# GpSimd's scatters in the first stage wait for the attention scores to leave TensorE

## The chip, the core and the metric

The kernel runs on one NeuronCore of one Trainium2 chip. A core has five engines with a queue of instructions each: TensorE (PE; its weight loads are a row of their own, PEld), VectorE (DVE), ScalarE (ACT), GpSimd (POOL) and SyncE (SP), which here only starts DMAs. Engines meet through semaphores: an instruction waits until a counter has reached a value, and every instruction behind it in the same queue waits with it. The metric is device time in microseconds of one launch; the time before is a median of three runs.

## The reference

The input `x` is 8192 tokens of 128 features (128 graphs of 64 nodes), `adj` a 64 x 64 matrix per graph.

```python
x = x + gnn0(layernorm(x), adj)            # adj @ (x @ W) + b
x = x + ffn0(layernorm(x))                 # attention, then a mixture of 8 experts
x = x + gnn1(layernorm(x), adj_normalised)
x = x + ffn1(layernorm(x))                 # 6 experts, top 2 of them

# inside ffn0, for every graph of 64 tokens, 4 heads of 32
scores = einsum("bhtd,bhsd->bhts", q, k) / sqrt(32)      # causal mask, softmax
x = x + (softmax(scores) @ v) @ wo.T
flat = rmsnorm(x)                          # root of the mean of squares
weights = top2(softmax(flat @ router_w.T)) # 2 of 8 experts for each token
out = sum over experts of weights * (silu(flat @ w1.T) * (flat @ w3.T)) @ w2.T
```

The first stage of the kernel computes everything up to `flat` and the choice of two experts for each token, and then copies every token's row of `flat` to two places in HBM, one for each expert chosen. The second stage runs the experts over those rows in blocks of 256. The third stage gathers the results and computes `gnn1` and `ffn1`.

## The kernel before

The tokens are cut into 16 groups of 512 (`NG = 16`), each of 4 tiles of 128. The first stage is a software pipeline written by hand: `sweep` (line 227 onwards holds the stage) runs a body 23 times on each engine, and in pass `i` the body works on group `i - k` for several depths `k` at once; `g[5]` in it means group `i - 5`. Each engine has its own list of steps and goes through them strictly in that order. Semaphores `at["name"]` say that step `name` of a group has ended, and `upto(name, n)` is the value that says so for the first n groups.

The steps that matter, by engine:

- TensorE, in order of a pass: `pk` (part of the projections to queries and keys, line 831), `prT` (transposes, line 901), `v` (line 871), `gnn` (lines 809 and 812), `rank` (lines 956 to 959), `y` (attention times values, 32 small matmuls of 64 x 66, line 919), `scores` (4 matmuls with the mask, line 885, then 64 small ones of 32 x 64, line 891), `hT` (line 823), `yT` (line 928), `gnnT` (line 796), `wo` (line 938), `pqs`, `pks`, `pq` (line 831).
- VectorE: `rden` and `yn` (lines 603 and 611, from `y`), `slot` (line 713, the rows in HBM that a group's tokens go to), `max` and `sub` (lines 589 and 597, first the maximum of the scores, then its subtraction), `lg` (line 642, needs `wo`), `nmr` (line 550, needs `rstd1`), `f2` (line 629), `topi` (line 656), `qks` and `qkc` (line 561), `ssv` (line 636, mean of squares), `qkr` (line 584). `max` waits for `scores`; `v` on TensorE waits for `qks`.
- ScalarE: `flat` (line 444, needs `rms`), `vd` (lines 402 to 405), `yTc` (line 426), `prTc` (line 419) among others.
- GpSimd: `rstd1` (line 314) and `rms` (line 319), two roots written as powers, and eight scatters for each group (line 329). One scatter is an indirect DMA that writes 128 rows of 512 bytes to the places that `slot` lists.

GpSimd's body runs in this order in pass `i`: scatters 2 and 5 of group `i - 6`, `rms` of group `i - 5`, scatters 1 and 7 of group `i - 6`, scatter 0 of group `i - 5` (the first of that group, which waits for its `flat` and `slot`), `rstd1` of group `i - 1`, scatters 3, 6 and 4 of group `i - 5`. The root that `nmr` needs therefore stands behind three scatters.

The last group's eight scatters are issued in the second stage, whose instructions start behind a barrier that all engines reach at the end of the first (line 227 and line 1274 in the order below).

Of the kernel before, what the change touches and what calls it, by code (L numbers as in the profile page):

```python
# [25 lines left out]
NG = TOK // GT  # L26
# [55 lines left out]
def signals(sem, names):  # L82

    return {n: sem(n) for n in names.split()}
# [12 lines left out]
def build(nc, x, adj_t, gnn0_w, gnn0_b, ln1, ln2, wqkv, wo, router0, w13, w2, gnn1_w, gnn1_b,  # L97
# [19 lines left out]
    with ExitStack() as whole:  # L117
# [31 lines left out]
        with ExitStack() as ctx:  # L149
# [51 lines left out]
            def upto(n, groups):  # L201

                return step_of[n].at(n, groups - 1)

            at, step_of = {}, {}
# [3 lines left out]
            def sweep(body):  # L209

                for i in range(NG + DEEP):
                    body([i - k if 0 <= i - k < NG else None for k in range(DEEP + 1)], [b for b in range(len(LN)) if LN_AT[b] == i])

            def tiles(a, g):

                return a[:, g * TG:(g + 1) * TG]
# [10 lines left out]
            with nc.Block() as block:  # L227
# [49 lines left out]
                @block.gpsimd  # L277
                def _(pool):
                    for i in range(2):
                        G.memset(adjt[i][:, :, :], 0.0).then_inc(zeroed, 1)  # L280
                        if i == 0:
                            G.memset(mhalf[:, :], -0.5).then_inc(pool_w, 1)
                            G.memset(one_raw[:, :], 0.0).then_inc(pool_w, 1)
                            G.memset(halves[:, :], 0.0).then_inc(pool_w, 1)
                    G.memset(zrow[:, :], 0.0).then_inc(zeroed, 1)
                    pool.wait_ge(pool_w, 3)
                    pool.wait_ge(zeroed, 3)
                    G.memset(one_raw[0:1, :], 1.0).then_inc(pool_w, 1)
                    pool.wait_ge(pool_w, 4)
                    G.memset(halves[0:NN, 7:8], 1.0).then_inc(pool_w, 1)  # L290
                    pool.wait_ge(pool_w, 5)
                    G.memset(one_raw[NN // 2:NN // 2 + 1, :], 1.0).then_inc(pool_w, 1)
                    pool.wait_ge(pool_w, 6)
                    G.memset(halves[NN:P, 15:16], 1.0).then_inc(pool_w, 1)
                    pool.wait_ge(pool_w, 7)
                    G.memset(sel_all[:, 0, TG, :], 0.0).then_inc(pool_w, 1)
                    G.memset(v_diag[:, :, :, :], 0.0).then_inc(pool_w, 1)
                    pool.wait_ge(pool_w, 9)
                    G.memset(v_diag[0:NN, :, :, 32:33], 1.0).then_inc(pool_w, 1)
                    pool.wait_ge(pool_w, 10)  # L300
                    G.memset(v_diag[NN:P, :, :, 65:66], 1.0).then_inc(pool_w, 1)
                    pool.wait_ge(pool_w, 11)

                    def ln_pow(bs):

                        for b in bs:
                            pool.wait_ge(at["ln_var"], upto("ln_var", b + 1))
                            s = slice(LN[b][0] * TG, (LN[b][-1] + 1) * TG)
                            G.tensor_tensor(rs_a[:, s], var_a[:, s], mhalf[:, s], ALU.pow).then_inc(at["ln_pow"], 1)

                    def rstd1(g):
                        if g is not None:
                            pool.wait_ge(at["var1"], upto("var1", g + 1))
                            G.tensor_tensor(rs_b[:, g, :, :], var_b[:, g, :, :], mhalf[:, 0:2 * TG].rearrange("p (k t) -> p k t", k=2), ALU.pow).then_inc(at["rstd1"], 1)

                    def rms(g):
                        if g is not None:
                            pool.wait_ge(at["ssv"], upto("ssv", g + 1))
                            G.tensor_tensor(tiles(rr2, g), tiles(ssv, g), mhalf[:, 0:TG], ALU.pow).then_inc(at["rms"], 1)

                    def scatter(n, g):

                        if g is not None and g < NG - 1:
                            if n == 0:
                                if g == 0:
                                    pool.wait_ge(zero_fill, 16 * (NDUM + NE0))
                                pool.wait_ge(at["flat"], upto("flat", g + 1))
                                pool.wait_ge(at["slot"], upto("slot", g + 1))
                            G.indirect_dma_start(  # L329
                                out=slots_in, out_offset=bass.IndirectOffsetOnAxis(ap=slot_now0[g % 2][:, n:n + 1], axis=0),  # L330
                                in_=flat[g % 2][:, n // 2, :], in_offset=None, bounds_check=ROWS - 1).then_inc(scattered[g % 2], 16)

                    def body(g, new):
                        ln_pow(new)
                        scatter(2, g[6])
                        scatter(5, g[6])
                        rms(g[5])
                        scatter(1, g[6])
                        scatter(7, g[6])
                        scatter(0, g[5])  # L340
                        rstd1(g[1])
                        scatter(3, g[5])
                        scatter(6, g[5])
                        scatter(4, g[5])
                    sweep(body)

                @block.scalar
# [678 lines left out]
        with ExitStack() as ctx:  # L1026
# [34 lines left out]
            upto = x2[:, :, :].rearrange("p t c -> p (t c)")[:, 0:MB * 8].rearrange("p (j e) -> p j e", e=8)  # L1061
# [40 lines left out]
            at = signals(sem, "pick held add0 add1 st0 mv0 var0 rstd0 scale xn xb aT tT gnn x3 "  # L1102
                              "st1 mv1 var1 rstd1 f3 f3T hi lo rh rhr logits "
                              "etop ep gateT gTc eb oTc oT ob")
# [1205 lines left out]
```

## Time and profile before

| | us |
|---|---|
| time, median of 3 runs (lowest to highest) | 863.1 (862.56 to 863.46) |
| profiled execution: span from first to last instruction | 932.6 |
| first stage in it | 0 to about 315 |
| second stage in it | about 315 to 590 |
| third stage in it | about 590 to 932 |
| TensorE busy in the span | 846.5 (91%) |
| GpSimd busy in the span | 433.0 (46%) |

The span is the profiled execution's own time on the core; the page gives none for what lies around it, so that the span alone stands beside the median. Every instruction of that execution left a record, which is not so in the runs that were timed. A start is when the engine began an instruction; an instruction that sat waiting has its idle time in square brackets, with what ended it: an engine and line, "remote" where nothing of this core in the trace fits, "issue" where nothing in it was waited for. The end of a matmul is modelled and not measured.

### The profile page before, as it was taken

How to read it: one execution, taken by the hardware profiler on the slowest of the kernel's cores; microseconds unless marked ns; L12 is line 12 of the kernel's file. 1: busy time of each engine (PE TensorE's matmuls, PEld its weight loads, DVE VectorE, ACT ScalarE, POOL GpSimd, SP SyncE). 2: the span in 40 equal slices, each digit the busy share in tenths (PEclk: the TensorE clock that was granted, in tenths of full speed). 3: DMA queues.
4: the chain of work that ended last, by engine and by line, in shares of the span. 5: the costliest groups of instructions: out<-in, count | busy, mean ns of one | idle time of the engine just before them, and what ended most of it. 6: DMA issues, size and time to landing. Idle time of an engine off the chain costs nothing.

```text
span 932.6 us, 21565 instructions
## 1 busy us (share of the span) xinstructions
PE 846.5 (91%) x6286; PEld 649.8 (70%) x6287; DVE 698.3 (75%) x2699; ACT 515.8 (55%) x1072; POOL 433.0 (46%) x410
## 2 busy tenths in 40 slices
PE   7988898989866499999999998999998999999998
PEld 6656676766643399999999998755665555555564
DVE  5898777767743499887777786988887778777763
ACT  3666666756532355665666554456555555545554
POOL 3258777668744630092010022366665556656400
PEclk9999989989977799999999999999999999999999
DMA  9504211131000376666666674144333333433322
GB/s 252 158 24 106 67 41 41 44 99 41 31 23 26 109 205 181 174 181 182 172 172 161 168 182 114 43 141 151 118 115 114 107 107 122 135 112 132 121 80 90
DMA packets 104712, 108.25 MB, mean 116 GB/s; under 512 B 27279, under 2 KB 88673, under 8 KB 102465
## 3 DMA queue, kind: packets, MB, share of 16 engines
q1 hardware_dynamic: 94096, 88.52, 33.3%
q0 software_dynamic: 8880, 18.19, 6.5%
q8 instruction: 36, 0.59, 0.3%
q10 hardware_dynamic: 1664, 0.66, 0.3%
q14 instruction: 36, 0.29, 0.1%
HBM read 82.07 MB, written 25.26 MB: 115 GB/s over the span
## 4 chain that ended last, share of the span: by engine, by line
PE 52%; issue 6%; DVE 3%; POOL 2%; another core or an unknown queue 1%; ACT 1%; DVEq 0%; POOLq 0%; ACTq 0%
PE banks L2041 15%; PE banks L2081 10%; PE banks L2207 7%; PE banks L2199 6%; PE banks L2175 5%; PE banks L2056 2%; PE banks L2113 2%; POOL expert_rows L1336 1%; PE banks L2102 1%; PE banks L2221 1%; PE banks L2130 1%; PE banks L2151 1%; PE banks L2122 1%; PE banks L2142 1%
## 5 line engine op out<-in xcount | busy, mean ns | idle before, releaser
L1336 POOL DMA_INDIRECT expert_rows<-slots_out,slot_c x128 | 143.8, 1124 | 80.9 <-DVE ys L1580 45.0
L329 POOL DMA_INDIRECT slots_in<-flat,slot_now x120 | 123.3, 1027 | 46.8 <-issue 34.6
L2041 PE MATMUL banks<-xT_hi,w_hi 128*128 128x256 f32 (+1 forms) x426 | 126.1, 296 | 0.7 <-issue 0.4
L2041 PE MATMUL banks<-xT_hi,w_lo 128*128 128x256 f32 (+1 forms) x426 | 120.1, 282 | 0.0
L2041 PE MATMUL banks<-xT_lo,w_hi 128*128 128x256 f32 (+1 forms) x426 | 119.8, 281 | 0.0
L2081 PE MATMUL banks<-w_sb,prod 128*128 (+1 forms) x852 | 106.7, 274 | 0.0
L2081 PEld LDWEIGHTS banks<-w_sb,prod 128*128 128x128 f32 (+1 forms) x852 | 101.0, 191 | 0.5 <-issue 0.2
L2041 PEld LDWEIGHTS banks<-xT_hi,w_hi 128*128 128x128 f32 (+1 forms) x426 | 75.6, 177 | 1.4 <-issue 1.4
L2041 PEld LDWEIGHTS banks<-xT_lo,w_hi 128*128 128x128 f32 (+1 forms) x426 | 75.8, 178 | 0.0
L2041 PEld LDWEIGHTS banks<-xT_hi,w_lo 128*128 128x128 f32 (+1 forms) x426 | 75.6, 177 | 0.0
L1401 ACT ACTIVATE w_hi<-w_raw 128x684 fp32r<-128x684 f32 x71 | 54.9, 773 | 29.1 <-PE banks L2041 24.5
L1410 ACT ACTIVATE xT_hi<-banks,ln 128x256 fp32r<-128x256 f32 x71 | 33.7, 474 | 57.0 <-PE banks L2056 56.3
L2175 PE MATMUL banks<-f_hi,ew_hi 128*128 128x512 f32 x96 | 64.2, 669 | 0.4 <-ACT h L1427 0.2
L831 PE MATMUL banks<-hT,wq 128*128 128x512 f32 x128 | 61.6, 622 | 2.7 <-DVE sc L597 2.7
L1599 DVE TENSOR_TENSOR w_lo<-w_raw,w_hi 128x684 fp32r<-128x684 f32 x71 | 63.0, 888 | 0.0
L1361 POOL TENSOR_TENSOR rs_d<-var_d,mhalf 128x4 f32<-128x4 f32 x16 | 17.9, 1121 | 93.8 <-DVE var_d L1744 93.8
L1434 ACT ACTIVATE flat<-banks,eb 128x512 f32<-128x512 f32 x64 | 43.8, 687 | 23.6 <-DVE ys L1772 15.6
L1416 ACT ACTIVATE act<-banks 128x512 f32<-128x512 f32 x71 | 42.6, 600 | 20.8 <-PE banks L2041 18.7
L1346 POOL TENSOR_TENSOR xb_c<-x,gb 128x512 f32<-128x512 f32 x16 | 20.6, 1285 | 70.5 <-DVE x L1672 70.1
L1608 DVE TENSOR_TENSOR prod<-banks,act 128x512 f32<-128x512 f32 x71 | 48.9, 688 | 0.3 <-PE banks L2041 0.3
L891 PE MATMUL banks<-qk_rot 32*64 32x64 f32 x1024 | 31.3, 239 | 19.3 <-issue 19.3
L589 DVE TENSOR_REDUCE mx<-banks 128x16 f32<-128x1024 f32 x16 | 19.5, 1222 | 37.5 <-remote 21.2
(303 smaller groups left out, 2187.9 us busy)
## 6 DMA issues: line engine op xcount, KB each, us to landing
f_all<-gates_dram SPq DMA_DIRECT2D x16, 1536.0 KB
w_raw<-in_w SPq DMA_DIRECT2D x71, 342.0 KB
xs<-slots_in SPq DMA_DIRECT2D x71, 128.0 KB
slots_out<-ys SPq DMA_DIRECT2D x71, 128.0 KB
base_all<-in_x SPq DMA_DIRECT2D x16, 256.0 KB, 4.2
out<-ob SPq DMA_DIRECT2D x16, 256.0 KB
slots_in<-zrow SPq DMA_DIRECT2D x20, 128.0 KB
adjt<-in_adj_t SPq DMA_DIRECT2D x32, 64.0 KB
```

The source lines that it names most:

```text
L329: G.indirect_dma_start(out=slots_in, out_offset=bass.IndirectOffsetOnAxis(ap=slot_now0[g % 2][:, n:n + 1], axis=0), in_=flat[g % 2][:, n / ...
L831: T.matmul(banks[bank][:, :], wq[:, n * P:(n + 1) * P], hT[:, :], start=True, stop=True).then_inc(done, 1)
L1336: G.indirect_dma_start(out=rows[p][:, n, :], out_offset=None, in_=slots_out[0:filled(g) * R, :], in_offset=bass.IndirectOffsetOnAxis(ap=sl ...
L1401: S.activation(w_hi[:, u % 2, :], w_raw[:, u, :], ACT.Copy).then_inc(w_hi_done, 1)
L1434: S.activation(h2[n % 3][:, :], banks[B_B[n]][:, :], ACT.Relu, bias=eb2[:, n:n + 1]).then_inc(per["rb"].sem, 1)
L1599: V.tensor_tensor(w_lo[:, u % 2, :], w_raw[:, u, :], w_hi[:, u % 2, :].bitcast(f32), ALU.subtract).then_inc(w_lo_done, 1)
L1608: V.tensor_tensor(prod[:, par, 0:2, :].rearrange("p c r -> p (c r)"), banks[3 + 3 * par][:, :], act1[:, par, 0:2, :].rearrange("p c r -> p ...
L2041: last = T.matmul(banks[bank][0:m, half * R:(half + 1) * R], ww[:, par, n * HIDP + c * P:n * HIDP + c * P + m], xx[:, par, :], start=q == ...
L2081: last = T.matmul(banks[7][:, t * P:(t + 1) * P], prod[0:widths[c], par, c, t * P:(t + 1) * P], w2_sb[0:widths[c], bass.ds(e * (KC * C) + ...
L2175: last = T.matmul(banks[B_A[n]][:, :], ww[:, w], ff[p][:, :], start=q == 0, stop=q == 2)
L2199: T.matmul(banks[B_B[n]][:, :], ew2[:, n * C:(n + 1) * C], h1[n % 3][:, :], start=True, stop=True).then_inc(per["b"].sem, 1)
L2207: T.matmul(banks[B_C][:, :], ew3[:, n * C:(n + 1) * C], h2g[n % 3][:, :], start=n == 0, stop=False).then_inc(per["c"].sem, 1)
```

## The change

A new step `behind_scores` is called between `rms` and the two scatters 1 and 7. In pass `i` it makes GpSimd wait until the `scores` step of group `i - 3` has ended (of the last group, once `i - 3` is past it). Nothing else is edited, and no instruction is added that computes or moves data.

```diff
+                    def behind_scores(g):
+
+                        if g is not None and g < NG - 1:
+                            pool.wait_ge(at["scores"], upto("scores", min(g + 3, NG - 1) + 1))
+
                     def body(g, new):
                         ln_pow(new)
                         scatter(2, g[6])
                         scatter(5, g[6])
                         rms(g[5])
+                        behind_scores(g[6])
                         scatter(1, g[6])
                         scatter(7, g[6])
                         scatter(0, g[5])
```

GpSimd's queue in the middle of the stage, one pass from `rms` on, first before the change (`rr` is written by `rms`, `rs_b` by `rstd1`; the brackets name semaphores waited for):

```order
L319 TENSOR_TENSOR rr<-ssv,mhalf 128x4 [waits at_ssv]
L329 DMA slots_in<-flat,slot_now 69632x128 x2
L329 DMA slots_in<-flat,slot_now 69632x128 [waits at_slotf,at_flat]
L314 TENSOR_TENSOR rs_b<-var_b,mhalf 128x8 [waits at_mv1]
L329 DMA slots_in<-flat,slot_now 69632x128 x5
```

The same pass after the change:

```order
L319 TENSOR_TENSOR rr<-ssv,mhalf 128x4 [waits at_ssv]
L329 DMA slots_in<-flat,slot_now 69632x128 [waits at_scores]
L329 DMA slots_in<-flat,slot_now 69632x128
L329 DMA slots_in<-flat,slot_now 69632x128 [waits at_slotf,at_flat]
L314 TENSOR_TENSOR rs_b<-var_b,mhalf 128x8 [waits at_mv1]
L329 DMA slots_in<-flat,slot_now 69632x128 x5
```

No instruction has moved against another; the first scatter behind `rms` has a wait, and the two scatters, the third one, `rstd1` and five more scatters are queued behind it.

GpSimd's queue at the end of the stage, where `rstd1` has no group left, before:

```order
L319 TENSOR_TENSOR rr<-ssv,mhalf 128x4 [waits at_ssv]
L329 DMA slots_in<-flat,slot_now 69632x128 x2
L329 DMA slots_in<-flat,slot_now 69632x128 [waits at_slotf,at_flat]
L329 DMA slots_in<-flat,slot_now 69632x128 x5
L319 TENSOR_TENSOR rr<-ssv,mhalf 128x4 [waits at_ssv]
L329 DMA slots_in<-flat,slot_now 69632x128 x2
L227 UNCONDITIONAL_BRANCH
L1274 UNCONDITIONAL_BRANCH [waits barrier_Pool_Activation_PE_DVE_SP_gather]
```

And after:

```order
L319 TENSOR_TENSOR rr<-ssv,mhalf 128x4 [waits at_ssv]
L329 DMA slots_in<-flat,slot_now 69632x128 [waits at_scores]
L329 DMA slots_in<-flat,slot_now 69632x128
L329 DMA slots_in<-flat,slot_now 69632x128 [waits at_slotf,at_flat]
L329 DMA slots_in<-flat,slot_now 69632x128 x5
L319 TENSOR_TENSOR rr<-ssv,mhalf 128x4 [waits at_ssv]
L329 DMA slots_in<-flat,slot_now 69632x128 [waits at_scores]
L329 DMA slots_in<-flat,slot_now 69632x128
L227 UNCONDITIONAL_BRANCH
L1280 UNCONDITIONAL_BRANCH [waits barrier_Pool_Activation_PE_DVE_SP_gather]
```

The order is again the same. In the last two passes the wait names scores that ended a pass or more earlier; in the two passes ahead of them it names the scores of the last two groups.

## Rows read from the trace of the kernel before

**Rows 1.** The page's head: span, and number of instructions recorded.

```profile
span 932.6 us, 21565 instructions
```

**Rows 2.** Stretches: length; busy us of PE, PEld, DVE, ACT, POOL (instructions); clock, DMA.

```profile
0.00:330.00 330.00, 269.91 (x2746) 201.71 (x2748) 225.56 (x974) 181.11 (x479) 202.55 (x194) 0.89 0.27 78
330.00:592.00 262.00, 258.91 (x2227) 257.88 (x2227) 213.82 (x445) 151.62 (x274) 52.86 (x52) 0.99 0.63 167
592.00:933.00 341.00, 317.68 (x1317) 190.23 (x1315) 258.94 (x1282) 183.10 (x320) 177.59 (x166) 0.99 0.36 114
```

**Rows 3.** Waits: who, for whom, us in total, times, longest.

```profile
ACT tT_c L1441 <- remote: 26.2, 8, 3.6
DVE mx L589 <- remote: 21.2, 2, 10.8
DVE mx L589 <- PE banks L891: 16.3, 6, 3.6
DVE rden L603 <- remote: 7.8, 5, 1.7
```

**Rows 4.** Timeline, TensorE, group 1: start, us, engine, line, operation, count.

```profile
39.98 1.01 PE L871 MATMUL banks<-wq,hT 128*128 128x72 f32 x8
...
44.11 0.91 PE L891 MATMUL banks<-qk_rot 32*64 32x64 f32 x64
```

**Rows 5.** Timeline, 203 to 222 us: scores of group 11, and what follows.

```profile
205.59 1.05 POOL L329 DMA_INDIRECT slots_in<-flat,slot_now  x1 [0.20 <-issue]
...
206.60 0.57 PE L891 MATMUL banks<-qk_rot 32*64 32x64 f32 x18
...
206.94 0.97 POOL L329 DMA_INDIRECT slots_in<-flat,slot_now  x1 [0.30 <-issue]
...
207.59 0.36 PE L891 MATMUL banks<-qk_rot 32*64 32x64 f32 x6 [0.42 <-issue]
...
208.33 0.74 PE L891 MATMUL banks<-qk_rot 32*64 32x64 f32 x40 [0.38 <-issue]
...
208.37 0.26 DVE L603 RECIPROCAL rden<-banks 128x16 f32<-128x16 f32 x1 [1.68 <-remote]
...
209.90 0.97 POOL L329 DMA_INDIRECT slots_in<-flat,slot_now  x1 [1.99 <-DVE slot_now L713]
...
210.89 1.68 POOL L314 TENSOR_TENSOR rs_b<-var_b,mhalf 128x8 f32<-128x8 f32 x1
...
212.61 0.16 DVE L550 SCALAR_TENSOR_TENSOR nmr<-mv_b,rs_b 128x4 f32<-128x4 f32 x1
...
214.75 1.21 DVE L561 TENSOR_TENSOR qk_sin<-banks,cst 128x1024 f32<-128x1024 f32 x1
...
216.37 1.01 PE L871 MATMUL banks<-wq,hT 128*128 128x72 f32 x8
```

**Rows 6.** Timeline, 247 to 294 us: scores of group 14, and the tail.

```profile
247.09 0.97 POOL L329 DMA_INDIRECT slots_in<-flat,slot_now  x1 [0.30 <-issue]
...
247.18 1.04 PE L901 MATMUL banks<-cst,pr 128*128 128x128 f32 x8
...
248.26 1.03 ACT L419 ACTIVATE prT<-banks 128x1024 f32<-128x1024 f32 x1 [0.60 <-issue]
...
252.41 0.94 PE L891 MATMUL banks<-qk_rot 32*64 32x64 f32 x43
...
252.45 1.05 POOL L329 DMA_INDIRECT slots_in<-flat,slot_now  x1 [0.20 <-issue]
...
261.48 0.97 POOL L329 DMA_INDIRECT slots_in<-flat,slot_now  x1 [0.30 <-issue]
...
263.93 1.23 DVE L589 TENSOR_REDUCE mx<-banks 128x16 f32<-128x1024 f32 x1 [10.80 <-remote]
...
293.45 1.04 POOL L319 TENSOR_TENSOR rr<-ssv,mhalf 128x4 f32<-128x4 f32 x1 [7.61 <-DVE ssv L636]
```

**Rows 7.** One line's instructions: duration ns min/median/max, first and last start, shape.

```profile
L329 POOL DMA_INDIRECT slots_in<-flat,slot_now x120: 968/975/1808, 60.4 to 310.9; - x120
```

## The prediction

> **What bounds the kernel now.** I read the head of the page first, against the times. The recorded execution spans 932.6 us [rows 1]; the median of the timed runs is 863.1, which is 69.5 less. So before any term is priced it has to be known which part of the trace the timed runs don't have.
>
> The stretches come next. TensorE is busy for 258.91 of 262 us in the second stretch and for 317.68 of 341 in the third [rows 2]. If the timed runs keep just that busy time, 576.6 us, they have at most 863.1 - 576.6 = 286.5 us for the first 330: at least 43.5 us of the first stretch is in the record only.
>
> The timeline of the first stage shows what that can be. Where no scatter is near, the 64 score matmuls take 0.91 us [rows 4]. In group 11 they start at 206.60 and end at 209.07, with two gaps of "issue", while GpSimd scatters; VectorE and ScalarE stand still, and `rden` comes 1.68 us late for a `y` that had ended before the scores began [rows 5]. In group 14 eight scatters run back to back from 252.45 to 262.45; 43 score matmuls go at full pace, and `max` starts at 263.93, after 10.80 us of waiting, once the last scatter is over [rows 6]. The table of waits adds this up: `max` waited 21.2 + 16.3 us and `rden` 7.8, together 45.3 us [rows 3]. That is nearly the 43.5 missing from the same stretch. The third stage has the like, 26.2 us, where ScalarE waits beside the gathers [rows 3].
>
> Is it the scatter alone that holds TensorE's signals back? No: at 247.09 one is under way, eight transposes end at 248.22, and ScalarE picks them up at 248.26 [rows 6]. What sets the scores apart is their density: 64 matmuls and as many weight loads, 128 records, in 0.91 us. I conclude, and no row proves it, that the stall is one of writing records while GpSimd issues DMAs, and that the timed runs have little of it.
>
> The Trainium skill, "NOTIFIC — the notification-queue block", section 7.1, speaks for that: the block that takes the records is set up so that its inner pipeline holds its producers back rather than lose one. By that rule the scores' stall goes with the recording and the sum below stands.
>
> The Trainium skill, "Runtime: NRT & Kernel Launch", section "The ~15µs preamble/postamble breakdown", speaks against it: a profile's total is about 6.2 us above the reported time for any kernel. By it the timed runs would hold nearly all the stalls. Here the gap is 69.5 us, so the measurement decides against the figure; the mechanism it implies is the first rival.
>
> **The change, part by part.** Nothing is computed or moved that was not before; one wait is added in each of 15 passes. Behind it in GpSimd's queue stand scatters 1 and 7, scatter 0, `rstd1`, five scatters and the next `rms`. VectorE's `nmr` waits for `rstd1`, and behind `nmr` stand `f2`, `qks`, `qkc` and `qkr`; TensorE's `v` waits for `qks`. That is the path on which the wait costs.
>
> Let s be the end of the scores.
>
> *After.* The first scatter starts about 0.20 after what released it, takes 1.05, the next two 0.30 + 0.97 each [rows 5, 7]: the third ends at s + 0.20 + 1.05 + 1.27 + 1.27 = s + 3.8. `rstd1` takes 1.68 and `nmr` follows by 0.04 [rows 5]: s + 5.55.
>
> *Before, without the stall.* Group 11's scores would end at 206.60 + 0.91 = 207.51. Everything behind the late `rden` moves up by its 1.68, so `nmr` at 212.61 becomes 210.93 [rows 5]: s + 3.4. The wait makes `nmr` 2.1 us late.
>
> *What of it is hidden.* `qk_sin` starts 2.14 after `nmr` and ends at 215.96, `v` starts at 216.37: TensorE was last there by 0.4, and that much lateness costs nothing [rows 5]. The rest is on the path.
>
> *The period of a group.* From `v` to the scores takes 44.11 - 39.98 = 4.13 [rows 4]; that group has no `rank`, for which I add 0.2. After: 5.55 + 2.14 + 1.21 + 0.05 + 4.3 + 0.91 = 14.15. Before, by the same path: 3.4 + (216.37 - 212.61) + 4.3 + 0.91 = 12.4. But GpSimd's own pass is longer than that: eight scatters 1.28 apart, 1.68 for `rstd1`, 1.05 for `rms` make 12.9 [rows 5 to 7]. I take 12.9. Each period grows by 14.15 - 12.9 = 1.25 us. The bounds: 1.75, if GpSimd runs a little faster than its records, and 0, if in the timed runs something unseen already makes the period 14.15.
>
> *How often.* `rstd1` stands behind the wait for groups 5 to 15. For group 5 the code still has statistics of new input between `max` and `sub` on VectorE, which I take to cover it. Ten periods remain: 12.5 us.
>
> *The tail.* In the last passes there is no `rstd1`; the wait only moves scatters. In group 14 the first one goes from 252.45 to 252.41 + 0.94 + 0.20 = 253.55, 1.1 us later [rows 6]. GpSimd is idle for 7.61 us before `rms` at 293.45 [rows 6], which looks like cover; but that idle time is there because `max` was 10 us late. Without the stall VectorE is ready before GpSimd is through its eight scatters, GpSimd's queue leads to the barrier at the stage's end, and the 1.1 us stays: 1 us, with bounds 0 and 2.
>
> *What it removes.* Scores that meet no scatter: worth at most the 45.3 us in the record, and by the above next to nothing in the timed runs. I take 0; the other end is in the first rival.
>
> Sum for the timed runs: 863.1 + 12.5 + 1 = 876.6, so 876.5. Sum against the profiled execution's own 932.6: there the stall is real, and goes. Of its 45.3 us the last `max` waited 21.2 - 10.8 = 10.4 [rows 3], but behind it GpSimd's eight scatters lead once the stall is gone: the `rms` at 293.45 can come earlier by its idle 7.61 less the 1.1 alone, 6.5 us, so 3.9 of the 10.4 are not given back. That makes 932.6 - 41.4 + 13.5 = 904.7. So the forecast is that the span falls by some 28 us while the time rises by 13.5.
>
> **The rivals.**
>
> *The stall is real in the timed runs.* For it: the record shows it where scores meet scatters, in the middle of the stage and in its tail [rows 5, 6], and the change takes away just that. Against it: the 43.5 us that the first stage must lose. If all of it were real the time would be 863.1 - 28 = 835. The turning point: with a share f of the 41.4 us real, the change gains as soon as 41.4 f is over 13.5, so from f = 0.33. By the stretches f is at most (45.3 - 43.5) / 45.3, under 0.1 [rows 2, 3], unless TensorE's modelled busy time in the other stages is itself stretched. Half real gives 863.1 - 20.7 + 13.5 = 856.
>
> *The lateness is hidden.* If GpSimd's scatters follow each other faster when nothing is recorded, `rstd1` is ready for `nmr` anyway. To bring 5.55 down to 3.4 + 0.4 the three scatters must shrink from 3.6 to 1.85 us, about half; 968 ns is the least in 120 records [rows 7], which speaks against it. Or VectorE or ScalarE bounds the period already. Time: 863 to 864.5.
>
> *The wait runs on into ScalarE.* GpSimd is through its five scatters at s + 5.5 + 0.2 + 6.4 = s + 12.1 and `rms` ends at 13.15. `flat` and the four `vd` copies follow on ScalarE ahead of `yTc`, which `wo` needs. That leaves them 1.0 us until the next scores end at 14.15, and `yTc` is wanted soon after. Nothing in the rows says how much of that is short; at half of the 1.0 us in ten groups, 5 us come on top: 882.
>
> **How the numbers follow.** The forecast with its third rival, which has the same sign, gets 0.70; its own range is ten times 0.5 to 1.75 plus 0 to 2, and some of the 5, so 868 to 885. The real stall gets 0.17, the hidden lateness 0.13. What a measurement of this kernel can tell from no change is about 0.2%, 1.7 us: faster 0.17, same 0.13, slower 0.70. The range of 861 to 885 takes in the forecast, the hidden lateness and the mildest of the real stall.
>
> **What would show it.** In the changed kernel's profile: score matmuls of every group in about 0.9 us without gaps; `max` soon after them in the last two groups; the first scatter behind `rms` waiting for the scores; `nmr` waiting for `rstd1` for 1 to 2 us in each middle group, where group 11's shows no wait now [rows 5]; a span near 905. A span that falls beside a time that rises would confirm that the stall was the recording's. I am wrong if the time falls below 861: then the scatters do hold the scores back in the timed runs too. I am also wrong if `nmr` finds `rstd1` ready, whatever the time.

## The result, and the profile after

The changed kernel takes 885.1 us (median of 4 runs, 882.5 to 888.7) against 863.3 (4 runs, 862.6 to 868.3): a ratio of 1.025, interval 1.021 to 1.029, so it is slower by some 22 us. The forecast was 876.5. The direction and the place were right, the size 9 us short: the time stands at the upper end of the range of 861 to 885.

The profiled execution of the changed kernel took 882.45 us, 2.05 more than its span of 880.4. It recorded 21565 instructions, as before. Its stretches, which answer to [rows 2], the first one cut 1.75 us behind the start of the first stage's last scatter (length; busy us of PE, PEld, DVE, ACT, POOL with instructions; granted clock of TensorE as a share of 2.4 GHz; DMA share; GB/s):

```profile
0.00:284.00 284.00, 233.88 (x2681) 172.88 (x2682) 215.11 (x946) 172.96 (x467) 186.73 (x177) 0.94 0.28 80
284.00:553.00 269.00, 263.57 (x2247) 261.45 (x2248) 218.52 (x455) 157.43 (x282) 64.14 (x66) 0.99 0.64 172
553.00:880.00 327.00, 319.38 (x1360) 194.74 (x1358) 262.39 (x1299) 184.60 (x324) 176.41 (x167) 1.00 0.37 120
```

The span fell by 52 us while the time rose by 22. The record of before is therefore no yardstick for the change; the first experiment replaces it.

The table of waits no longer has `max` waiting 21.2 + 16.3 us, `rden` 7.8, nor the third stage's `tT_c` behind a remote releaser [rows 3]. One entry is new and one has grown (who, line, for whom: us in total, times, longest; the second stood at 0.3 us in the first record of before and at 3.6 in the second, below):

```profile
POOL slots_in L329 <- PE banks L897: 23.3, 12, 4.0
...
DVE nmr L556 <- POOL rs_b L314: 17.5, 10, 3.0
```

The first is the added wait, the second its effect: ten times, as the forecast counted, VectorE stands before `nmr` until GpSimd has the root. One period of the timeline shows both (start, length, engine, line, operation; in brackets the idle time before it and its releaser; lines behind 329 are 6 higher than in before):

```profile
197.59 0.91 PE L897 MATMUL banks<-qk_rot 32*64 32x64 f32 x64
...
199.32 1.05 POOL L329 DMA_INDIRECT slots_in<-flat,slot_now  x1 [1.51 <-PE banks L897]
...
200.68 0.97 POOL L329 DMA_INDIRECT slots_in<-flat,slot_now  x1 [0.30 <-issue]
...
201.95 0.97 POOL L329 DMA_INDIRECT slots_in<-flat,slot_now  x1 [0.30 <-issue]
...
202.76 0.19 DVE L648 TENSOR_TENSOR lg<-banks,v_logits 128x32 f32<-128x32 f32 x1 [1.26 <-PE banks L944]
...
202.95 1.68 POOL L314 TENSOR_TENSOR rs_b<-var_b,mhalf 128x8 f32<-128x8 f32 x1
...
204.65 0.17 DVE L556 SCALAR_TENSOR_TENSOR nmr<-mv_b,rs_b 128x4 f32<-128x4 f32 x1 [1.70 <-POOL rs_b L314]
...
206.78 1.21 DVE L567 TENSOR_TENSOR qk_sin<-banks,cst 128x1024 f32<-128x1024 f32 x1
...
208.05 1.11 PE L877 MATMUL banks<-wq,hT 128*128 128x72 f32 x8 [1.02 <-DVE qk_sin L567]
...
212.40 0.91 PE L897 MATMUL banks<-qk_rot 32*64 32x64 f32 x64
```

Read it downwards as a chain: the scores end at 198.50, the first scatter starts 0.82 later, the third ends at 202.92, the root at 204.63, `nmr` follows 0.02 behind it, then the sine, then `v` on TensorE, which waits for the sine, then the next scores at 212.40. The period is 14.81 us, and groups 7 to 13 repeat it within 0.02. The scores meet no scatter and take 0.91, against 2.47 with two gaps in [rows 5].

### The profile page after: what moved, and what is told of

It is laid out like the page before. It is cut to its first block, busy times and chain, and to the rows that moved or that the text cites. A ratio compares the mean times of both kernels' runs of the same rounds, so it can differ in the third digit from the quotient of the medians.

```text
span 880.4 us, 21565 instructions
## 1 busy us (share of the span) xinstructions
PE 816.8 (93%) x6286; PEld 629.1 (71%) x6287; DVE 696.0 (79%) x2699; ACT 515.0 (58%) x1072; POOL 427.3 (49%) x410
## 4 chain that ended last, share of the span: by engine, by line
PE 62%; issue 2%; DVE 1%; POOL 1%; ACTq 0%; ACT 0%; POOLq 0%; DVEq 0%
PE banks L2047 16%; PE banks L2087 10%; PE banks L2213 9%; PE banks L2205 9%; PE banks L2181 7%; PE banks L2062 2%; PE banks L2119 2%; PE banks L2108 1%; PE banks L2136 1%; PE banks L2227 1%; PE banks L2148 1%; PE banks L2128 1%; PE banks L2157 1%; POOL expert_rows L1342 1%; PE banks L2219 0%
## 5 line engine op out<-in xcount | busy, mean ns | idle before, releaser
L329 POOL DMA_INDIRECT slots_in<-flat,slot_now x120 | 125.9, 1049 | 58.4 <-issue 34.8
L1586 DVE COPY ys<-banks 128x256 f32<-128x256 f32 x71 | 29.9, 421 | 23.2 <-PE banks L2087 22.8
L1602 DVE SCALAR_TENSOR_TENSOR xT_lo<-banks,ln,xT_hi 128x256 fp32r<-128x256 f32 x71 | 34.2, 482 | 16.6 <-ACT xT_hi L1416 16.4
```

The costliest lines, as they stand in the source:

```text
L329: G.indirect_dma_start(out=slots_in, out_offset=bass.IndirectOffsetOnAxis(ap=slot_now0[g % 2][:, n:n + 1], axis=0), in_=flat[g % 2][:, n / ...
```

## The experiments

Below, s is the end of a group's score matmuls.

### The kernel before, recorded again

> The kernel before once more, for a second recorded execution. If the stalls of the scores belonged to that one recorded execution, this one has score matmuls of 0.91 us in every group, a period near 12.9 us in the middle of the first stage and a span near 861. If every recorded execution has them, the span is near 930 again with the scores at 2.5 to 5 us. The time is near 863 either way.

It took 867.2 us with a span of 865.2. The same program, so no edit; and the long stalls of the first record are gone, though the scores don't come down to 0.91 nor the period to 12.9:

```profile
186.57 1.40 PE L891 MATMUL banks<-qk_rot 32*64 32x64 f32 x64
...
186.95 1.05 POOL L329 DMA_INDIRECT slots_in<-flat,slot_now  x1 [0.19 <-issue]
...
190.57 1.68 POOL L314 TENSOR_TENSOR rs_b<-var_b,mhalf 128x8 f32<-128x8 f32 x1
...
192.28 0.16 DVE L550 SCALAR_TENSOR_TENSOR nmr<-mv_b,rs_b 128x4 f32<-128x4 f32 x1 [0.38 <-POOL rs_b L314]
...
195.81 1.01 PE L871 MATMUL banks<-wq,hT 128*128 128x72 f32 x8
...
197.10 1.22 DVE L584 TENSOR_TENSOR qk_rot<-qk_cos,qk_sin 128x1024 f32<-128x1024 f32 x1
...
197.62 1.55 POOL L329 DMA_INDIRECT slots_in<-flat,slot_now  x1 [0.30 <-issue]
...
199.19 1.05 POOL L319 TENSOR_TENSOR rr<-ssv,mhalf 128x4 f32<-128x4 f32 x1
...
200.05 1.40 PE L891 MATMUL banks<-qk_rot 32*64 32x64 f32 x64
```

Beside a scatter the scores take 1.40 us: 0.49 more than alone, not 1.5 or 10 more. `nmr` comes at s + 4.31 and waits 0.38; the period is 13.48. What sets it can be followed in these rows. GpSimd has no idle time but the 0.2 to 0.3 between instructions, and VectorE none that the view shows between `nmr` and `qkr`. From one `rms` (at 185.71) to the end of the root behind the three scatters are 6.54 us, then 0.03 to `nmr`, 4.82 to `qkr`, 1.22 for `qkr`, 0.85 from its end to the end of the scatter ahead of the next `rms`, and 0.02: together 13.48. Neither the scores nor `v` are in this ring. `v` doesn't wait for the sine here, and behind the scores TensorE waits another 0.58 us for `vd`. The stretches, the first again cut 1.7 us behind the start of the last scatter, say what is left to compare with the changed kernel:

```profile
0.00:268.00 268.00, 230.32 (x2681) 170.97 (x2682) 216.06 (x946) 173.86 (x467) 187.94 (x177) 0.96 0.30 85
268.00:537.00 269.00, 263.46 (x2239) 261.09 (x2240) 217.63 (x453) 156.73 (x280) 63.73 (x66) 0.99 0.65 172
537.00:865.00 328.00, 320.17 (x1368) 195.92 (x1367) 263.35 (x1302) 185.31 (x325) 176.37 (x167) 1.00 0.37 119
```

The last two stretches are 597 us here and 596 in the changed kernel, the first is 268 and 284: the whole difference between the kernels is made in the first stage, 16 us in these two records. 41 timed runs of before, beside the experiments, had spans between 859.4 and 866.8; none was near 932.6. That execution was the exception. The recorded executions of this run (867.2) and of the changed kernel (882.45, the shortest of its four) are themselves among the timed ones, so what the text ahead of the prediction says of the timed runs, that not every instruction leaves a record, does not hold for them: recording does not stretch a program so in general.

### The root's place, without the wait

```diff
                         scatter(0, g[5])
-                        rstd1(g[1])
                         scatter(3, g[5])
                         scatter(6, g[5])
+                        rstd1(g[1])
                         scatter(4, g[5])
```

> The kernel before, without any wait for the scores, but with rstd1 two scatters later in GpSimd's pass (behind scatter 6 instead of scatter 0). GpSimd's pass is as long as before. Theory A: nmr comes 2.5 us later, near 6 us after the scores' end, the period is some 14.5 us and the time about 879. Theory B: the late root costs nothing, as GpSimd loses no time: 863 to 865.

Made in the kernel before, this costs nearly all that the change costs: 881.7 us, ratio 1.020 (1.016 to 1.024). No wait is added, the scores still may meet scatters, and `nmr` now waits for the root:

```profile
DVE nmr L550 <- POOL rs_b L314: 25.9, 11, 3.1
```

So a late root is enough to make a loss of this size. It is more than the ten even steps I expected: the periods alternate, 13.7 and 17.8, and this is not the root alone. In a short pass `v` to scores takes 4.35 us at the full granted clock; in the long one, where TensorE had waited 2.26 us for the sine, it takes 7.31 at a mean of 0.53, nearly all of it at the 1.2 GHz level:

```profile
194.72:199.07 4.35, 4.35 (x59) 3.69 (x59) 4.35 (x15) 2.83 (x8) 3.08 (x3) 1.00 0.46 179
209.75:217.06 7.31, 7.31 (x58) 6.31 (x58) 4.95 (x20) 3.70 (x10) 4.48 (x4) 0.53 0.09 29
```

So 3 us of every second pass are the slower clock. How much of the 881.7 the lateness alone would make, this run does not say.

### The root straight behind the wait

```diff
                         behind_scores(g[6])
+                        rstd1(g[1])
                         scatter(1, g[6])
                         scatter(7, g[6])
                         scatter(0, g[5])
-                        rstd1(g[1])
```

> The changed kernel with rstd1 straight behind the wait, ahead of the three scatters. Theory A (the wait costs because rstd1 stands three scatters behind it, so that nmr is late): nmr is ready by 3.4 us after the scores' end again, the period goes back to about 13 and the time to about 865. Theory B (the wait costs because GpSimd's pass is full: rms ends later, and flat, the vd copies and yTc on ScalarE with it): rms still ends some 14 us after the last scores, the period is 14.3 instead of 14.8, and the time about 880.

The time stays, and theory A's 865 does not come: 882.5 us, ratio 1.023 (1.018 to 1.027). The root is early, `nmr` at s + 3.10 in every second pass, but the passes between are long: periods of 12.25 and 18.45, a mean of 15.35. In the long ones VectorE stands in front of `lg`, the step ahead of `nmr`, and waits for `wo`:

```profile
195.97 1.05 POOL L319 TENSOR_TENSOR rr<-ssv,mhalf 128x4 f32<-128x4 f32 x1
...
197.05 1.28 ACT L450 ACTIVATE flat<-f_all,rr 128x128 f32<-128x128 f32 x4 [3.91 <-POOL rr L319]
...
201.70 2.02 PE L944 MATMUL banks<-wo_sb,yT 128*128 128x136 f32 x8
...
203.76 0.19 DVE L648 TENSOR_TENSOR lg<-banks,v_logits 128x32 f32<-128x32 f32 x1 [5.24 <-PE banks L944]
203.86 0.15 DVE L556 SCALAR_TENSOR_TENSOR nmr<-mv_b,rs_b 128x4 f32<-128x4 f32 x1
```

This is the chain of my third rival (the root of the sum of squares, then `flat`, `vd`, `yTc`, `wo`). With eight scatters behind the root it is what comes last. The clock has a part here too: the granted clock is 0.82 over the long pass and 1.00 over the short one, and `wo` takes 2.02 us in place of 1.15. So moving the root forward is no cure, and the rival is real, though not what the changed kernel shows, where `lg` at 202.76 is done 1.7 us before `nmr` can start.

### The wait in the tail alone

```diff
-                        if g is not None and g < NG - 1:
+                        if g is not None and NG - 5 <= g < NG - 1:
                             pool.wait_ge(at["scores"], upto("scores", min(g + 3, NG - 1) + 1))
```

> The changed kernel with the wait only in the last four passes that have it (scatter groups 11 to 14), where rstd1 has no group behind it. Theory A: 1.1 us of GpSimd's tail, time about 864. Theory B: GpSimd is full in the tail as well and its end sets the stage's end, 865 to 867. If most of the loss were in the tail, it would be near 880.

864.6 us (10 runs), ratio 1.002 (1.000 to 1.005): 0 to 4 us, near the 1 us of the forecast. From the end of group 13's scores to the last scatter's start it took 53.0 us, against 51.4 in the second record of before: 1.6 more with the wait.

### One scatter less behind the wait

```diff
-                        behind_scores(g[6])
                         scatter(1, g[6])
+                        behind_scores(g[6])
                         scatter(7, g[6])
```

> The changed kernel with the wait one scatter later: scatter 1 goes ahead without it, 7 and 0 and all behind them wait for the scores. Theory A, the price is the root's lateness: scatter 7 starts 0.8 us behind the scores, 0 at s+2.2, the root at s+3.2 and nmr at s+4.9, where the kernel before has 4.3 and the changed one 6.15. The scores meet one scatter and take about 1.2 in place of 1.40. The period is 13.48 + 0.6 - 0.2 - 0.1 = 13.8, and the time 863 + 10 x 0.3 + 1 = 867, ratio 1.004 (1.001 to 1.009). Rival, the wait itself costs (queue restarted once a pass, whatever stands behind it): nearly the whole 22 us stay, 880 or more. Rival, scores that meet no scatter were worth something that only the full wait brings: then this one is as good as before or faster, 858 to 863.

869.9 us, ratio 1.0088 (1.0071 to 1.0105): within the interval given, at its upper end. `nmr` is where theory A put it, 4.79 behind the scores; the scores keep their 1.41 us, where I had expected 1.2: one scatter beside them costs as much as before.

```profile
185.88 1.41 PE L897 MATMUL banks<-qk_rot 32*64 32x64 f32 x64
...
186.30 1.05 POOL L329 DMA_INDIRECT slots_in<-flat,slot_now  x1 [0.20 <-issue]
...
188.09 0.97 POOL L329 DMA_INDIRECT slots_in<-flat,slot_now  x1 [0.74 <-ACT flat L450]
...
190.37 1.68 POOL L314 TENSOR_TENSOR rs_b<-var_b,mhalf 128x8 f32<-128x8 f32 x1
...
192.08 0.16 DVE L556 SCALAR_TENSOR_TENSOR nmr<-mv_b,rs_b 128x4 f32<-128x4 f32 x1 [0.83 <-POOL rs_b L314]
...
199.82 1.40 PE L897 MATMUL banks<-qk_rot 32*64 32x64 f32 x64
```

The view names `flat` as releaser of the scatter at 188.09; it starts 0.80 behind the scores' end, as behind the added wait elsewhere. The rival that the wait itself costs (880 or more) is out: the wait is there in each pass, and two thirds of the loss are gone.

### A shorter root, in both kernels

`nmr` needs only half of the 8 columns; the other half gives a ratio close to 1, here the first term of its series on VectorE:

```diff
-    G.tensor_tensor(rs_b[:, g, :, :], var_b[:, g, :, :], mhalf[:, 0:2 * TG]..., ALU.pow)
+    G.tensor_tensor(rs_b[:, g, 1, :], var_b[:, g, 1, :], mhalf[:, 0:TG], ALU.pow)
...
-    V.reciprocal(tiles(inv_h, g), rs_b[:, g, 1, :])
+    V.reciprocal(tiles(inv_h, g), var_b[:, g, 0, :])
...
-    V.tensor_tensor(tiles(ratio, g), rs_b[:, g, 0, :], tiles(inv_h, g), ALU.mult)
+    V.tensor_scalar(tiles(ratio, g), tiles(inv_h, g), -0.5e-5, 1.0 + 0.5e-6, ALU.mult, ALU.add)
```

In the kernel before:

> The kernel before with rstd1 on 4 columns instead of 8 (the other root follows from the first through a reciprocal and one VectorE operation in place of another; with the variances here it agrees to single precision). Theory A': GpSimd's pass, which shows no idle time in the second recorded execution of the kernel before, sets the period of 13.48 us, so 0.62 us less for the root gives 12.86, ten times: 857. Rival: TensorE's own chain of about 13.4 us sets it: 863.

861.9 us (10 runs), ratio 0.9964 (0.9942 to 0.9986): a gain of 1 to 5 us, less than expected, and the only version here that beats both kernels. `nmr` is 0.53 earlier, the period 13.09, 0.39 shorter for a root that is 0.63 shorter; then `nmr` no longer waits for the root, but `lg` ahead of it for `wo`, and the gain ends:

```profile
189.12 0.19 DVE L642 TENSOR_TENSOR lg<-banks,v_logits 128x32 f32<-128x32 f32 x1 [0.85 <-PE banks L938]
189.23 0.20 DVE L550 SCALAR_TENSOR_TENSOR nmr<-mv_b,rs_b 128x4 f32<-128x4 f32 x1
```

In the changed kernel:

> The changed kernel, with the root on 4 columns in place of 8 (the other half, which only feeds a ratio, comes from a reciprocal on VectorE). Theory A, the loop scores, scatters 1, 7, 0, root, nmr, sine, v, scores sets the period: the root is 0.47 us shorter (as it was in the kernel before: nmr 1.24 behind the root's start in place of 1.71), nmr at s+5.7, the period 14.80 - 0.47 = 14.3, and over eleven periods some 5 us off the changed kernel's 885: 880, ratio 1.019. Rival B, GpSimd's whole pass with the root of the sum of squares, flat, vd, yTc and wo behind it sets it: the scatters behind the short root end 0.6 earlier too, so the period falls by the same 0.5, but wo then still waits and lg for it, as it did where the root came early: passes alternate and the mean stays over 14.8, 885. Rival C, the period is set on TensorE and the wait only shows there: no change, 885.

876.2 us, ratio 1.0165 (1.0148 to 1.0182), so some 7 of the 22 us come back. The root takes 1.05 in place of 1.68, and the period falls from 14.81 to 14.17, by 0.64 for 0.63 of the root: theory A, somewhat more than I had expected of it. No pass alternates (rival B), and rival C is out.

```profile
193.85 0.91 PE L897 MATMUL banks<-qk_rot 32*64 32x64 f32 x64
...
199.21 1.05 POOL L314 TENSOR_TENSOR rs_b<-var_b,mhalf 128x4 f32<-128x4 f32 x1
...
200.29 0.16 DVE L556 SCALAR_TENSOR_TENSOR nmr<-mv_b,rs_b 128x4 f32<-128x4 f32 x1 [1.07 <-POOL rs_b L314]
...
208.02 0.91 PE L897 MATMUL banks<-qk_rot 32*64 32x64 f32 x64
```

### More work for GpSimd

A memset of 0.54 us (512 columns) goes into GpSimd's queue in each pass: `G.memset(idle[:, :], 0.0)`. First in the kernel before, behind the root, ahead of scatter 4:

```diff
                         scatter(6, g[5])
+                        extra(g[6])
                         scatter(4, g[5])
```

> The kernel before with one memset of 128x512 (0.54 us in the trace, some 0.6 to 0.7 with its gap) more in each pass of GpSimd, behind the root, into a tile that nothing reads. Theory A': GpSimd's pass sets the period, so each of some ten periods and a few passes of the tail grow by 0.6: 869 to 871. Rival (TensorE's chain sets it): 863 to 865.

865.3 us (10 runs), ratio 1.001 (0.999 to 1.004), period 13.49: nothing. GpSimd's pass looked full, with no idle time but the 0.2 to 0.3 between instructions, and yet it took up half a microsecond:

```profile
191.91 0.55 POOL L339 MEMSET idle<- 128x512 f32 x1
...
195.27 1.07 POOL L330 DMA_INDIRECT slots_in<-flat,slot_now  x1 [0.30 <-issue]
...
196.36 1.05 POOL L320 TENSOR_TENSOR rr<-ssv,mhalf 128x4 f32<-128x4 f32 x1
```

The last scatter ahead of `rms` takes 1.07 here and 1.55 in the second record of before, where it starts 0.52 behind `qkr`'s start on VectorE; here it starts 1.01 behind it (`qkr` at 194.26). Begun earlier it takes longer and ends at the same place, 0.85 behind the end of `qkr` in both records. So the end of GpSimd's pass hangs on VectorE's `qkr`, and there was room for the memset ahead of it. The part of the pass from `rms` to the root, which the ring above also holds, was not tested so.

In the changed kernel, in the same place:

> The changed kernel with the same memset behind the root. Theory A (the loop is scores, wait, three scatters, root, nmr, qks, v, scores): GpSimd waits 1.5 us in each pass anyway and takes the memset out of that; the period stays 14.80 and the time 883 to 886. Theory B (rms ends later, and flat, vd and yTc with it, and these are what makes the scores late): 0.6 us more per period, 889 to 892.

886.2 us, ratio 1.025 (1.021 to 1.029), period 14.80: nothing, as expected of a queue that waits 1.5 us in every pass. And straight behind the wait, ahead of the root:

> The changed kernel with the same memset straight behind the wait, ahead of the three scatters and the root. Theory A: nmr comes 0.6 to 0.7 us later after the scores in each of some ten periods: 890 to 893, with GpSimd's wait still there at the same length. Theory B: the same total pass as with the memset behind the root, so the same time as that kernel.

884.8 us, ratio 1.025 (1.021 to 1.029), period 14.82. Here theory A promised 0.6 us per pass, and that was a miss. The timeline has the reason:

```profile
200.19 0.53 POOL L344 MEMSET idle<- 128x512 f32 x1 [0.75 <-PE banks L907]
...
200.95 1.05 POOL L330 DMA_INDIRECT slots_in<-flat,slot_now  x1 [0.23 <-issue]
```

The memset starts 0.07 behind the scores' end, the scatter 0.83 behind it, and 0.82 without the memset. The first scatter behind a wait has a lead of 0.8 us anyway, and the memset lies inside it. The root's start is the same, s + 4.45, so the run agrees with the loop after all, but it could not test it.

## Why the prediction was right in kind and short in size

All from the timeline of one steady group, in us behind s:

| kernel | root starts | `nmr` starts | scores last | period | period less `nmr` |
|---|---|---|---|---|---|
| before, short root | 2.55 | 3.78 | 1.07 | 13.09 | 9.31 |
| before | 2.60 | 4.31 | 1.40 | 13.48 | 9.17 |
| wait one scatter later | 3.08 | 4.79 | 1.41 | 13.94 | 9.15 |
| changed, short root | 4.45 | 5.53 | 0.91 | 14.17 | 8.64 |
| changed | 4.45 | 6.15 | 0.91 | 14.81 | 8.66 |

The last column only adds up what follows `nmr` (to `v`, to the next scores, and the scores themselves), and so comes out whatever sets the period. That the loop through the scores, the root, `nmr`, the sine and `v` sets it is shown for the last three rows: there TensorE waits for the sine in front of `v` (0.38 for its weights, 0.39 and 1.02), and the scores release the scatters. In the first two rows `v` does not wait for the sine, and nothing on GpSimd waits for the scores.

*The path of the wait: right.* Root, `nmr`, `qks`, `v`, ten times. In the changed kernel a root that is 0.63 shorter makes the period 0.64 shorter, and a scatter moved ahead of the wait brings `nmr` 1.36 earlier and the period 0.87 down, with scores that are 0.50 longer. The late root alone, without the wait, costs nearly the same (881.7), there in part by the clock.

*The two periods: each some 0.6 too short, and their difference nearly right by luck.* After, I had 14.15 and it is 14.81: the first scatter starts 0.82 and not 0.20 behind the scores. I took the lead from a scatter behind another GpSimd instruction [rows 5, 7]. The scatter at 209.90 in [rows 5], which did wait, had the longer one: the step that it waits for ends at 209.05, 0.85 earlier.

```profile
208.91 0.14 DVE L713 CAST slot_now<-slots_f 128x8 uint32<-128x8 f32 x1
```

Before, I had "GpSimd's own pass is 12.9", and it is 13.48: the scatter beside `qkr` takes 1.55 and not 0.97, which makes up the 0.58. As the memset shows, that is no bound of GpSimd's own work; its pass, `nmr` and VectorE up to `qkr` bound before together. So a period grows by 1.33, where I had 1.25.

*The lateness: its two ends wrong too, its size nearly right.* I put `nmr` at s + 5.55 after and s + 3.4 before; it is 6.15 and 4.31, so 1.84 us late, where I had 2.1. `v` starts 3.53 behind `nmr` before and 3.39 after: 0.14 was hidden, not 0.4.

*"What it removes: 0": not shown to be wrong as a price, wrong in its reason.* I concluded that the stall of the scores belongs to the record. The stalls of 1.5 to 10 us do go with that one execution, for a cause that stays open, but in recorded executions of 864.7 to 867.2 us a scatter still costs the scores 0.49 a group, some 5 of the 41 us of the first rival. In the loop of the changed kernel that counts. In the kernel before, the 0.58 that TensorE waits for `vd` behind the scores could take it up; no run there has the scores shorter and all else equal.

*The total, where the forecast fell short.* Ten periods at 1.33 are 13.3, where I had 12.5. The tail cost 2.7 (54.1 us from group 13's scores to the last scatter, 51.4 before), where I had 1. Another 4.0 us, for which the sum had no term, are lost between the scores of groups 3 and 6 beyond the loop's 1.33 each, measured against the record with the wait in the tail alone. Of these, 2.4 are a gap in the scores of group 4, with GpSimd idle after `rms`:

```profile
89.13 1.05 POOL L319 TENSOR_TENSOR rr<-ssv,mhalf 128x4 f32<-128x4 f32 x1
```

```profile
89.53 0.83 PE L897 MATMUL banks<-qk_rot 32*64 32x64 f32 x54
92.80 0.50 PE L897 MATMUL banks<-qk_rot 32*64 32x64 f32 x10 [2.44 <-issue]
```

The second record of before has the like in that group, 3.42 us; the record with the wait in the tail alone has none, and a span 2.6 us shorter. The other 1.5 are the granted clock: behind the scores of group 5 it takes 5.84 us from `v` to the next scores, and 4.34 a pass later. TensorE had waited 1.12 us for the sine there and 2.33 a pass later, so the wait alone does not tell when the clock falls:

```profile
117.77:123.61 5.84, 5.84 (x58) 5.14 (x59) 4.95 (x20) 3.31 (x10) 3.93 (x4) 0.71 0.11 37
134.06:138.40 4.34, 4.34 (x58) 3.69 (x58) 4.34 (x15) 2.07 (x5) 3.70 (x4) 1.00 0.13 45
```

In the tail the clock differs as well: 0.85 over the 54.1 us, 0.93 over the 51.4, and 0.89 over the 53.0 of the record with the wait in the tail alone. So not all of the 2.7 need be GpSimd's lead.

The timed runs of both kernels spread over some 7 us (861.4 to 868.9 and 882.5 to 888.7), four times the 1.7 that I took for what can be told apart, and the longer ones have the lower mean clock. Of the 41 of before, 28 runs at 0.985 to 0.987 have a median of 862.5 us, 13 at 0.981 to 0.983 one of 866.9; of the changed kernel, two at 0.977 and 0.979 took 882.5, two at 0.968 and 0.972 took 887.7 and 888.7. Whether the gap brings the clock down or something else does is not shown, and some 2 us of the median's 21.9 remain without a place.

*Small slips in the prediction.* Its terms for `nmr` after the change add up to s + 5.52, and eight scatters, the root and `rms` as priced there to 12.97. The 43 matmuls of group 14 that "go at full pace" take 0.94 us, as long as 64 do elsewhere. None of these changes the sum by more than 0.1 us a group.

*The signs I gave.* Scores of 0.91 in all groups but 4 and 14, `max` at once in the last two, the scatter's wait and the 1.70 of `nmr` all came. The span did not: 880.4 and not 905, because I took the excess of one execution (in the second record the first stage's last scatter starts 44.6 us earlier, and the rest is 22.8 shorter) for what every recording adds. I had written that a falling span beside a rising time would confirm that the stall was the recording's. It does not: the same program, recorded again, lost the excess without any change. The subtraction that bounded it, at least 43.5 us of the first stage, was sound. What stretched that execution stays open.

## What to carry to other kernels

A wait in an in-order queue is priced by the first thing behind it that another engine needs: follow that result around the loop to the next wait, and compare its lateness with the slack there, which was 0.14 us here. What bounded the pass before need not be on that path, so price both loops, and check the granted clock before a longer pass is put down to a wait. Where the span of a record and the timed median disagree by per cents, record the same program again before reading any stall in it as either real or an artefact. An engine without idle time need not be the bound; 0.5 us of extra work on it is a cheap test, which speaks for that place in the pass alone.

## What the runs showed of the hardware

- An indirect DMA on GpSimd behind a wait for TensorE starts 0.8 us after the matmuls' end (0.85 behind VectorE's `slot_now` in the first record of before), a memset in the same place 0.07. A memset of 0.53 us put in front of the DMA does not delay it.
- An indirect DMA that runs beside VectorE's `qkr` (two inputs of 128 x 1024) ends 0.84 to 0.86 us behind the end of `qkr`, whenever it began: 0.30, 0.52 or 1.01 behind `qkr`'s start it takes 1.77 (with the shorter root), 1.55 (before) or 1.07 (with the memset).
- A scatter beside 64 small matmuls with their weight loads costs them 0.49 us where it starts 0.4 us into them (1.40 for 0.91), and 0.16 where it starts together with them (1.07, with the shorter root).
- The score matmuls of group 4 can stop on "issue" for 2.44 us with no scatter under way (the changed kernel), right behind 3 us in which the DMA engines were fully busy. In the second record of before they stop there for 3.42, beside three scatters. In all seven records that have this gap (0.75 to 3.42) it stands behind the 54th of the 64 matmuls. So a gap of this kind beside a scatter is no proof that the scatter made it; what makes it stays open. The granted clock of TensorE then fell to 0.50, the 1.2 GHz level, for the stretch behind the gap:

```profile
86.00:89.00 3.00, 2.20 (x45) 1.84 (x43) 2.37 (x9) 0.86 (x3) 2.50 (x3) 1.00 1.10 235
...
93.50:97.00 3.50, 3.50 (x18) 3.50 (x18) 2.42 (x3) 1.14 (x3) 2.24 (x3) 0.50 0.07 23
```
